# A gated cross-attention and expert layer: root steps of three norms on GpSimd, another order of A's transfers, another softmax path for pair 0, and sixteen leading products

## The chip, the cores and the metric

One core of a Trainium2 chip. The metric is the device time of one execution in microseconds (us), the median of three. Engines: TensorE (PE, with PEld for its weight loads), VectorE (DVE), ScalarE (ACT), GpSimd (POOL) and SyncE (SP), which here only issues transfers.

## The reference

For each of 16 batches x is 128 x 1024 (channels by positions) and ctx is 128 x 1024. What is computed:

```
xn  = layernorm(x)                      # over the 1024 positions
q   = Wq xn,  k = Wk ctx,  v = Wv ctx   # 8 heads of 64, hidden 512
qh  = softmax(q, over the 64 of a head) / 8
kh  = softmax(k, over the 1024 positions)
o   = Wo (heads: (kh v^T)^T qh) + bo
x  += tanh(g_xattn) * o / |o|_channels * g * sqrt(128)
y   = layernorm(x)
gates = softmax over the 16 largest of y Wr^T (64 experts), 0 elsewhere
x  += tanh(g_ffn) * 2 * sum_experts gates * B (A y)     # rank 16 each
```

All of it is float32 in accuracy: each product is made of three matmuls of float32r parts (high x high, low x high, high x low), so every matrix exists as a "hi" and a "lo" tile.

## The kernel before, in words

The program has two stages, with an order for each engine written out by hand; engines meet only at semaphores. The attention stage is a function `body(b, head, tail, ahead)` on every engine, called for b = 0 to 16: the "head" part works on batch b, the "tail" part ends batch b-1, and "ahead" loads and prepares batch b+1. Batches 0, 1, 14, 15 and 16 are written out, 2 to 13 are a loop (GpSimd splits its loop at 5 and 13). "Body 14" below is the call with b = 14. The second stage (`ffn_body`) takes the experts, one batch after another.

In a body TensorE makes k in four blocks of 128 hidden rows (`mm_k(b, 0..3)`, into banks 0 and 1) and q in four pairs of position blocks (`mm_q(b, 0..3)`, into banks 2 and 3). Each has one buffer, so the next product waits for the exponential of the one before. For k: VectorE takes the maximum (`max_k`, L868), ScalarE the exponential (`exp_k`, L586), TensorE transposes it (`tr_k`, L1284), ScalarE copies it to hi (L617) and VectorE makes lo (`lo_k`, L895). For q the softmax is over 64 neighbours, with 16 maxima to a pair (`max_q`, L874). A pair in `SHIFTED` (1 and 2 before) gets its maxima subtracted by two matmuls of the identity with the negated maxima, added onto q in PSUM (`shift_q`, L1274), and then one exponential of 128x1024 (L595). The other pairs (0 and 3 before) get 16 exponentials of 128x64, each with its maximum as bias (L602). GpSimd then halves the rows (`halve`, L391), VectorE sums (`sum_q`, L879), GpSimd multiplies (`normalise`, L398), TensorE transposes (`tr_q`, L1293), ScalarE and VectorE make hi and lo (L610, L888).

The tail: `context(b-1)` (24 matmuls of ekT by ctxT), copied to hi by ScalarE (`hi_kc`, L623) and lo by VectorE (`lo_kc`, L900), `fold` (12 matmuls of 128x256 with the folded Wv and Wo), `scale_m` (L912), `mt_hi`, `mt_lo` on GpSimd (L476), and `output` (two halves of 12 matmuls). The order on TensorE in a body before:

```
context(b-1, 0); mm_q(b, 0); context(b-1, 1); mm_k(b, 1); shift_q(b, 0)
tr_q(b-1, 1); fold(b-1); mm_q(b, 1); mm_k(b, 2); tr_k(b, 0); output ...
```

(`shift_q(b, 0)` did nothing, as pair 0 was not shifted.) On ScalarE the first 8 exponentials of pair 0 stood before `hi_kc`, the other 8 behind it.

The norms |o| of a batch are found from squares: the norms of batches 0 to 2 together, in body 14. TensorE sums them (`sum_early`), then VectorE takes an inverse root in 11 steps on 128x96 tiles (`early_norms`, L846 to L854: a clamp, a bit trick for the first guess, 3 Newton rounds of 3), spread over body 14 in five places. `spread` (L864) broadcasts the roots, GpSimd multiplies and adds (`spread_first` L436, `add_first` L446). For later batches VectorE does the same on 128x32 tiles in the second stage (`norm_u`).

For the second stage the weights are loaded while the attention ends: A's high parts by eight converting transfers of 544 KB on GpSimd's queue (`hi_a`, L419; t = 0 to 2 in body 15, 3 and 4 at its end, 5 to 7 in body 16 behind `halve(15, 3)`), over buffers of the attention stage, so t >= 3 waits for the last q product and the last transpose of k. B's parts (`b_raw`, L311, L316), u and x come on SP's queue, also in body 16. The first product of the second stage, `up(0, 0)` (L60 to L62, aT by yT), stands in body 16 behind `fold(15)` and waits for all of A and for `lo_y(0)` (L1013). `lo_y(0)` waits for `add_first(1)`.

Of the kernel before, what the change touches and what calls it, by code (L numbers as in the profile page):

```python
# [6 lines left out]
def flamingo_layer(nc, x, ctx, ctxT, g_xattn, g_ffn, WqT, WkT, Wv, WoT, bo, g, AT, BT, u_dram, out):  # L7
# [8 lines left out]
    NB, C, N = x.shape  # L16
# [24 lines left out]
    SHIFTED = (1, 2)  # L41
# [45 lines left out]
    with outer:  # L87
# [126 lines left out]
        n_part, n_sum, n_step, n_spread = sem("n_part"), sem("n_sum"), sem("n_step"), sem("n_spread")  # L214
        u_done, x2_done = sem("u_done"), sem("x2_done")
# [133 lines left out]
        def _(pool):  # L349
# [80 lines left out]

            def spread_first(e):
# [25 lines left out]
            def body(b, head, tail, ahead, split=False):  # L457
# [4 lines left out]
                if tail and not head:  # L462
                    for t in range(5, DC):
                        hi_a(t)
# [13 lines left out]
                if split:  # L478
                    lo_a(b - SPLIT)
                if head and not ahead:  # L480
                    add_first(0)
# [17 lines left out]
                if head and not ahead:  # L499
                    add_first(1)  # L500
                if head:
                    halve(b, 2)
                if head and not ahead:
                    for t in range(3, 5):
                        hi_a(t)

# [40 lines left out]
        def _(act):  # L547
# [42 lines left out]
            def exp_q(b, p, halves=(0, 1)):  # L590
# [8 lines left out]
                for h in halves:  # L599
# [89 lines left out]
            def body(b, head, tail, ahead, early=False):  # L689
# [6 lines left out]
                if head and started(b):  # L696
                    exp_q(b, 0, (0,))
# [5 lines left out]
                if head:  # L703
# [5 lines left out]
                    exp_q(b, 0, (1,) if started(b) else (0, 1))  # L709
# [98 lines left out]
        def _(dve):  # L808
# [48 lines left out]
            def early_norms(steps):  # L857
                for k in steps:
                    norm_step(k, 1, psN_early.rearrange("p (e n) -> p e n", e=EARLY), EARLY, 0)

            def spread(slot, dst, steps):

                dve.wait_ge(n_step, steps)
# [176 lines left out]
            def norm_u(e):  # L1040

                before = NRT * (e - EARLY + 1)
# [3 lines left out]
                spread(0, rb, before + NRT)  # L1046
# [13 lines left out]
            def body(b, head, tail, ahead, early=False):  # L1060
# [9 lines left out]
                if last:  # L1070
                    dve.wait_ge(ctx_lo, 2 * NB)
                    spread(0, rb_first[0], NRT)
                if ahead and started(b):
                    stats(b + 1)
                if head and started(b):
                    max_q(b, 0)
                if tail:
                    sum_q(b - 1, 3)
                if early:
                    part_early(b - 2)  # L1080
                if ahead and started(b):
                    std(b + 1, range(5))
# [477 lines left out]
```

## Time and profile before

| | |
|---|---|
| median of 3 runs | 977.32 us (974.84, 977.32, 977.46) |
| the profiled execution, its own time | 975.75 us |
| its span, first to last instruction | 974.1 us |
| mean granted TensorE clock | 0.992 |
| busy: PE, DVE, ACT, POOL | 928.2, 708.3, 531.6, 464.9 us |
| attention stage with the change-over, until the first product of the second stage | about 566 us |
| one body in the loop | 33.0 us |

Busy times are sums over the span and do not say what a stage waits for; for that the timelines of one body and the waits are read. A matmul's own duration is modelled to its end, and the next one starts before it: the distance of two starts is what one costs.

### The profile page before, as it was taken

The page shows a single profiled execution, that of the slowest core. Times are in us where ns is not written, and L with a number is a line of the kernel's source. Part 1 is how long each engine was busy: PE and PEld are TensorE (multiplying, and loading weights), DVE is VectorE, ACT ScalarE, POOL GpSimd, SP SyncE. Part 2 cuts the span into 40 slices and gives each one's busy share as a digit, 9 for nine tenths or more (in the row PEclk, how much of TensorE's full clock was granted, in tenths as well). Part 3 has the DMA queues.
Part 4 walks back from the last instruction along what each step waited for, and adds up shares of the span by engine and source line. Part 5 has one row for each costly group of instructions (what it writes and reads, how often), then busy time and mean ns, then how long its engine had stood idle before and what let it go on. Part 6 is the DMA issues. An engine that isn't in the chain of part 4 may idle for free.

```text
span 974.1 us, 16214 instructions
## 1 busy us (share of the span) xinstructions
PE 928.2 (95%) x5036; PEld 790.3 (81%) x5036; DVE 708.3 (73%) x1541; ACT 531.6 (55%) x1214; POOL 464.9 (48%) x311
## 2 busy tenths in 40 slices
PE   4899999999999999999989779999999999999998
PEld 3687777788887878787858679999999999999986
DVE  5888888878888888888897738766666666666621
ACT  5888887788878887887867624222222222222100
POOL 3665656677777867785757824311111111111100
PEclk9999999999999999999999989999999999999999
DMA  4216221232223122311311754111111111111001
GB/s 151 87 65 233 103 104 47 87 131 72 101 87 131 65 93 103 131 65 46 127 62 51 252 231 151 66 65 66 65 66 67 65 65 65 64 58 51 22 22 43
DMA packets 24805, 88.30 MB, mean 91 GB/s; under 512 B 3264, under 2 KB 3264, under 8 KB 24768
## 3 DMA queue, kind: packets, MB, share of 16 engines
q1 hardware_dynamic: 19296, 67.91, 19.1%
q0 software_dynamic: 5184, 19.40, 6.1%
q10 hardware_dynamic: 288, 0.52, 0.2%
q8 instruction: 20, 0.33, 0.1%
q14 instruction: 17, 0.14, 0.0%
HBM read 71.04 MB, written 16.78 MB: 90 GB/s over the span
## 4 chain that ended last, share of the span: by engine, by line
PE 64%; DVE 15%; ACT 10%; issue 8%; POOL 1%; DMA 1%; DVEq 0%; ACTq 0%; POOLq 0%
PE ps L60 18%; PE ps L62 18%; PE ps L61 18%; ACT qe L602 7%; PE ps L1284 3%; PE ps L1293 3%; DVE kmax L868 3%; DVE qT_lo L888 2%; DVE qtop L874 2%; DVE ekT_lo L895 2%; PE ps L1387 1%; PE ps L1358 1%; DVE mt L912 1%; DVE std_t L81 1%; ACT qT_hi L610 1%
## 5 line engine op out<-in xcount | busy, mean ns | idle before, releaser
L452 POOL TENSOR_TENSOR rb<-u_in,rb 128x1024 f32<-128x1024 f32 x14 | 33.7, 2408 | 260.1 <-DVE rb L864 260.1
L398 POOL TENSOR_TENSOR qe<-qe,qrec 128x1024 f32<-128x1024 f32 x64 | 121.3, 1905 | 54.5 <-DVE qrec L882 54.5
L60 PE MATMUL ps<-aT_hi,yT_hi 128*128 128x448 f32 (+2 forms) x384 | 128.2, 334 | 9.0 <-issue 9.0
L62 PE MATMUL ps<-aT_lo,yT_hi 128*128 128x448 f32 (+2 forms) x384 | 126.5, 329 | 0.0
L61 PE MATMUL ps<-aT_hi,yT_lo 128*128 128x448 f32 (+2 forms) x384 | 126.4, 329 | 0.0
L602 ACT ACTIVATE qe<-ps,qtop 128x64 f32<-128x64 f32 x512 | 111.3, 377 | 27.6 <-DVE qtop L874 27.6
L888 DVE TENSOR_TENSOR qT_lo<-ps,qT_hi 128x512 fp32r<-128x512 f32 x128 | 82.5, 686 | 51.8 <-ACT qT_hi L610 51.3
L391 POOL TENSOR_TENSOR qhalf<-qe 128x512 f32<-128x512 f32 x64 | 82.0, 1282 | 69.5 <-ACT qe L602 69.3
L60 PE MATMUL ps<-bT_hi,hT_hi 128*128 128x512 f32 x256 | 102.5, 400 | 0.0
L62 PE MATMUL ps<-bT_lo,hT_hi 128*128 128x512 f32 x256 | 99.9, 390 | 0.0
L61 PE MATMUL ps<-bT_hi,hT_lo 128*128 128x512 f32 x256 | 99.7, 390 | 0.0
L682 ACT ACTIVATE hT_hi<-ps 128x512 fp32r<-128x512 f32 x32 | 19.1, 597 | 143.8 <-PE ps L1387 143.8
L617 ACT ACTIVATE ekT_hi<-ps 128x512 fp32r<-128x512 f32 x128 | 70.5, 607 | 31.7 <-PE ps L1284 31.3
L586 ACT ACTIVATE ek<-ps,kmax 128x1024 f32<-128x1024 f32 x64 | 72.7, 1135 | 20.6 <-DVE kmax L868 20.6
L610 ACT ACTIVATE qT_hi<-ps 128x512 fp32r<-128x512 f32 x128 | 69.6, 598 | 24.0 <-PE ps L1293 24.0
L60 PEld LDWEIGHTS ps<-aT_hi,yT_hi 128*128 128x128 f32 x384 | 73.0, 190 | 11.6 <-issue 9.2
L895 DVE TENSOR_TENSOR ekT_lo<-ps,ekT_hi 128x512 fp32r<-128x512 f32 x128 | 81.2, 676 | 1.0 <-ACT ekT_hi L617 1.0
L868 DVE TENSOR_REDUCE kmax<-ps 128x1 f32<-128x1024 f32 x64 | 77.5, 1210 | 1.9 <-PE ps L62 1.9
L1293 PE MATMUL ps<-ident,qe 128*128 128x128 f32 x512 | 69.7, 278 | 6.6 <-DVE ekT_lo L895 6.0
L1293 PEld LDWEIGHTS ps<-ident,qe 128*128 128x128 f32 x512 | 58.0, 141 | 21.7 <-issue 12.2
L61 PEld LDWEIGHTS ps<-aT_hi,yT_lo 128*128 128x128 f32 x384 | 73.1, 190 | 2.3
L62 PEld LDWEIGHTS ps<-aT_lo,yT_hi 128*128 128x128 f32 x384 | 73.0, 190 | 2.0
(148 smaller groups left out, 2358.6 us busy)
## 6 DMA issues: line engine op xcount, KB each, us to landing
x_in<-in_x SPq DMA_DIRECT2D x16, 512.0 KB, 4.4
ctx_in<-in_ctx SPq DMA_DIRECT2D x16, 512.0 KB, 4.9
ctxT_in<-in_ctxT SPq DMA_DIRECT2D x16, 512.0 KB, 3.3
ctxT_hi<-in_ctxT POOLq DMA_DIRECT2D x16, 512.0 KB, 3.7
u_scratch<-osb SPq DMA_DIRECT2D x16, 512.0 KB, 3.8
out<-res SPq DMA_DIRECT2D x16, 512.0 KB, 2.8
x<-in_x SPq DMA_DIRECT2D x15, 512.0 KB, 3.9
u_in<-u_scratch SPq DMA_DIRECT2D x14, 512.0 KB, 3.2
```

Of the source, the lines that this page charges most:

```text
L60: nc.tensor.matmul(psum, whi, mhi, start=start, stop=False)
L61: nc.tensor.matmul(psum, wlo, mhi, start=False, stop=False)
L62: return nc.tensor.matmul(psum, whi, mlo, start=False, stop=stop)
L391: nc.gpsimd.tensor_tensor(qhalf[:, p % 2, :].rearrange("p (h d) -> p h d", d=DH // 2), v[:, :, 0:DH // 2], v[:, :, DH // 2:DH], ALU.add).t ...
L398: nc.gpsimd.tensor_tensor(v, v, w, ALU.mult).then_inc(q_norm, 1)
L586: nc.scalar.activation(ek[:, j % 2, :].rearrange("p (a n) -> p a n", a=HF), psK, ACT.Exp, bias=kmax[:, j:j + 1], accum_out=ksum[:, j:j + 1 ...
L602: last = nc.scalar.activation(qe[:, p, HD * h + DH * n:HD * h + DH * n + DH], psQ[:, h, v], ACT.Exp, bias=qtop[:, p % 2, H * h + n:H * h + ...
L610: nc.scalar.activation(qT[0][:, :, n * P:n * P + P], psT[:, h, :].rearrange("p (j n) -> p j n", n=P), ACT.Copy).then_inc(q_hi, 1)
L868: nc.vector.tensor_reduce(kmax[:, j:j + 1], psK, axis=AX.XY, op=ALU.max, negate=True).then_inc(k_max, 1)
L888: nc.vector.tensor_tensor(qT[1][:, :, v], psT[:, h, :].rearrange("p (j n) -> p j n", n=P), qT[0][:, :, v].bitcast(f32), ALU.subtract).then ...
L895: nc.vector.tensor_tensor(ekT[1][:, n, w], psT[:, h, :].rearrange("p (n d) -> p n d", d=P), ekT[0][:, n, w].bitcast(f32), ALU.subtract).th ...
L1293: last = nc.tensor.transpose(psT[:, h, j * P:j * P + P], qe[:, p, w:w + P], ident[:, :])
```

## The change

- Pair 0 joins the shifted pairs: two matmuls and one 128x1024 exponential instead of 16 small ones; pair 3 alone keeps the bias form. On TensorE both halves of `context(b-1)` now stand together at the head of a body, before `mm_q(b, 0)`; `shift_q(b, 0)` now works, behind `mm_k(b, 1)`. On VectorE `max_q(b, 0)` moves from before `sum_q(b-1, 3)` to behind `lo_kc(b-1)`; in body 16 `lo_kc(15)` moves ahead of `sum_q(15, 3)`; `part_early` stands before the first `std` steps.
- The early root: VectorE makes the clamp and the first guess in one place, and GpSimd the three rounds, 4 steps each (12 steps on 128x96), behind `mt_lo` of body 14 and ahead of `normalise(14, 0)`. `spread` waits for these. GpSimd's body 14 is now written out.
- A's transfers 3 to 7 are issued together at the end of GpSimd's body 15, and `add_first(1)` comes behind them instead of before `halve(15, 2)`.
- TensorE's program begins with 16 matmuls of the identity with itself, 128x512 each, into a bank that is not yet used.

```
-    SHIFTED = (1, 2)
+    WARM = 16
+    SHIFTED = (0, 1, 2)
GpSimd:
+            def early_newton():
+                s, r, t = ns[:, :, :], nr[:, :, :], nt[:, :, :]
+                pool.wait_ge(n_guess, 2)
+                for k in range(4 * NEWTON):
+                    if k > 0:
+                        pool.wait_ge(n_newton, k)
+                    if k % 4 == 0:
+                        last = nc.gpsimd.tensor_tensor(t, r, s, ALU.mult)
+                    elif k % 4 == 1:
+                        last = nc.gpsimd.tensor_tensor(t, t, r, ALU.mult)
+                    elif k % 4 == 2:
+                        last = nc.gpsimd.tensor_scalar(t, t, -0.5, 1.5, ALU.mult, ALU.add)
+                    else:
+                        last = nc.gpsimd.tensor_tensor(r, r, t, ALU.mult)
+                    last.then_inc(n_newton, 1)
...
-                if tail and not head:
-                    for t in range(5, DC):
-                        hi_a(t)
...
+                if isinstance(b, int) and b == NB - 2:
+                    early_newton()
...
-                if head and not ahead:
-                    add_first(1)
                 if head:
                     halve(b, 2)
                 if head and not ahead:
-                    for t in range(3, 5):
+                    for t in range(3, DC):
                         hi_a(t)
+                    add_first(1)
...
-            with pool.Fori(SPLIT + DC, NB - 1) as b:
+            with pool.Fori(SPLIT + DC, NB - 2) as b:
                 body(b, head=True, tail=True, ahead=True)
+            body(NB - 2, head=True, tail=True, ahead=True)
ScalarE:
-                if head and started(b):
-                    exp_q(b, 0, (0,))
                 if tail:
                     hi_kc(b - 1)
...
-                    exp_q(b, 0, (1,) if started(b) else (0, 1))
+                    exp_q(b, 0)
VectorE:
+            def early_guess():
+                s, r = ns[:, :, :], nr[:, :, :]
+                dve.wait_ge(n_sum, 1)
+                nc.vector.tensor_scalar(s, psN_early.rearrange("p (e n) -> p e n", e=EARLY), MIN_SS, None,
+                                        ALU.max).then_inc(n_guess, 1)
+                dve.wait_ge(n_guess, 1)
+                first_root(r, s).then_inc(n_guess, 1)
...
-                if head and started(b):
-                    max_q(b, 0)
-                if tail:
-                    sum_q(b - 1, 3)
                 if early:
                     part_early(b - 2)
-                if ahead and started(b):
-                    std(b + 1, range(5))
-                if norms:
-                    early_norms(range(2))
-                if tail:
-                    lo_kc(b - 1)
+                if norms:
+                    early_guess()
+                if ahead and started(b):
+                    std(b + 1, range(5))
+                if tail and head:
+                    sum_q(b - 1, 3)
+                if tail:
+                    lo_kc(b - 1)
+                if tail and not head:
+                    sum_q(b - 1, 3)
                 if head and started(b):
+                    max_q(b, 0)
                     max_k(b, 1)
...
-                if norms:
-                    early_norms(range(2, 4))
-                if norms:
-                    early_norms(range(4, 7))
...
TensorE:
                 if tail:
                     context(b - 1, 0)
+                    context(b - 1, 1)
                 if head:
                     if not started(b):
                         pe.wait_ge(wq_low, 1)
                     mm_q(b, 0)
-                if tail:
-                    context(b - 1, 1)
-                if head:
                     mm_k(b, 1)
                     shift_q(b, 0)
...
             pe.wait_ge(id_ready, 3)
+            for k in range(WARM):
+                nc.tensor.matmul(psX[:, 0, :], ident_r[:, :], ident_r[:, :].unsqueeze(1).broadcast_to([P, 4, P]),
+                                 start=True, stop=True)
```

The counts of semaphores are changed to fit (`n_guess`, `n_newton`; `norm_u` and `sum_u` no longer count the early steps).

## Rows read from the trace of the kernel before

**Rows 1.** The page, part 1: busy us (share of the span) x instructions.

```profile
PE 928.2 (95%) x5036; PEld 790.3 (81%) x5036; DVE 708.3 (73%) x1541; ACT 531.6 (55%) x1214; POOL 464.9 (48%) x311
```

**Rows 2.** Windows by stage: one loop body, body 14, body 15, start of body 16.

```profile
308.00:341.00 33.00, 32.41 (x178) 26.64 (x177) 27.70 (x49) 26.78 (x68) 24.70 (x18) 1.00 0.27 96
...
473.60:512.90 39.30, 34.06 (x179) 26.79 (x178) 36.39 (x60) 27.42 (x68) 21.73 (x15) 0.99 0.27 91
...
512.90:546.50 33.60, 31.95 (x171) 26.29 (x170) 27.95 (x46) 25.20 (x64) 26.01 (x18) 0.97 0.20 68
...
546.50:565.80 19.30, 9.21 (x55) 7.74 (x54) 11.74 (x30) 9.77 (x26) 12.03 (x11) 0.84 1.04 360
```

**Rows 3.** Timeline of the start: start us, us, engine line op [idle before <-releaser].

```profile
1.32 0.29 POOL L352 TENSOR_SCALAR_AFFINE_SELECT ident<-ident 128x128 f32<-128x128 f32 x1 [0.24 <-POOL ident L350]
...
9.72 0.77 PE L60 MATMUL ps<-ctx_hi,wk_hi 128*128 128x512 f32 x1 [9.72 <-POOL ctx_lo L362]
...
16.77 0.42 PE L62 MATMUL ps<-ctx_lo,wk_hi 128*128 128x512 f32 x1
...
17.42 3.39 ACT L602 ACTIVATE qe<-ps,qtop 128x64 f32<-128x64 f32 x16 [1.46 <-DVE qtop L874]
...
21.96 0.50 PE L60 MATMUL ps<-ctx_hi,wk_hi 128*128 128x512 f32 x1
```

**Rows 4.** Groups of instructions by line: busy us, mean ns.

```profile
L595 ACT ACTIVATE qe<-ps 128x1024 f32<-128x1024 f32 x32 | 33.0, 1030 | 0.0
```

**Rows 5.** Timelines of the loop body with b = 9: PE, ACT, DVE.

```profile
308.33 0.49 PE L60 MATMUL ps<-ekT_hi,ctxT_hi 128*128 128x512 f32 x1
...
312.38 0.50 PE L60 MATMUL ps<-wq_hi,xn_hi 128*128 128x512 f32 x1 [0.37 <-ACT qe L602]
...
319.47 0.28 PE L62 MATMUL ps<-wvo_lo,kc_hi 128*128 128x256 f32 x1
...
316.23 0.65 ACT L623 ACTIVATE kc_hi<-ps 128x512 fp32r<-128x512 f32 x1
...
313.38 1.23 DVE L874 TENSOR_REDUCE qtop<-ps 128x16 f32<-128x1024 f32 x1 [1.09 <-PE ps L62]
...
316.91 0.69 DVE L900 TENSOR_TENSOR kc_lo<-ps,kc_hi 128x512 fp32r<-128x512 f32 x1 [0.59 <-ACT kc_hi L623]
...
319.90 1.40 DVE L912 TENSOR_TENSOR mt<-ps,krec 64x512 f32<-64x512 f32 x2
```

**Rows 6.** The chain of waits in the loop: start us, us, what.

```profile
331.82 0.43 PE ps L1274 x2
```

**Rows 7.** Timelines of body 14: PE, DVE, POOL.

```profile
502.48 1.17 PE L1284 MATMUL ps<-ident,ek 128*128 128x128 f32 x8 [1.47 <-DVE qT_lo L888]
...
511.50 1.72 PE L1293 MATMUL ps<-ident,qe 128*128 128x128 f32 x8 [2.86 <-DVE ekT_lo L895]
...
498.83 2.32 DVE L854 SCALAR_TENSOR_TENSOR nr<-nt,nr 128x96 f32<-128x96 f32 x1
...
487.24 1.28 POOL L476 TENSOR_TENSOR mt_lo<-mt,mt_hi 128x512 fp32r<-128x512 f32 x1 [2.05 <-ACT mt_hi L627]
...
492.23 1.90 POOL L398 TENSOR_TENSOR qe<-qe,qrec 128x1024 f32<-128x1024 f32 x1 [3.71 <-DVE qrec L882]
...
494.94 2.52 POOL L362 TENSOR_TENSOR ctx_lo<-ctx_in,ctx_hi 128x512 fp32r<-128x512 f32 x2 [0.27 <-ACT ctx_hi L562]
...
498.66 2.37 POOL L375 TENSOR_TENSOR ctxT_lo<-ctxT_in,ctxT_hi 128x1024 fp32r<-128x1024 f32 x1
```

**Rows 8.** Timelines of the change-over: POOL, DVE, PE.

```profile
549.48 1.14 POOL L419 DMA_DIRECT2D aT_hi<-in_AT  x2
...
553.43 1.64 POOL L419 DMA_DIRECT2D aT_hi<-in_AT  x3
...
556.13 1.28 DVE L1013 TENSOR_TENSOR yT_lo<-ps,yT_hi 128x512 fp32r<-128x512 f32 x2
...
565.82 0.71 PE L60 MATMUL ps<-aT_hi,yT_hi 128*128 128x448 f32 x1 [9.05 <-issue]
```

More of the change, by code:

```diff
@@ L214, in flamingo_layer @@
         n_part, n_sum, n_step, n_spread = sem("n_part"), sem("n_sum"), sem("n_step"), sem("n_spread")
+        n_guess, n_newton = sem("n_guess"), sem("n_newton")
         u_done, x2_done = sem("u_done"), sem("x2_done")
@@ L588, in exp_k, with exp_q @@
                                      accum_out=ksum[:, j:j + 1]).then_inc(k_exp, 1)
-            def exp_q(b, p, halves=(0, 1)):
+            def exp_q(b, p):
                 if started(b):
@@ L598, in exp_q @@
                 act.wait_ge(q_max, 4 * b + p + 1)
-                for h in halves:
+                for h in range(2):
                     for n in range(H):
@@ L855, in norm_step, with spread @@
                 last.then_inc(n_step, 1)
[L857 to L863, printed above, removed]
+            def early_guess():
[5 more added lines that the diff above has]
+                first_root(r, s).then_inc(n_guess, 1)
+            def spread(slot, dst, *done):
+                dve.wait_ge(*done)
                 nc.vector.transpose(dst[:, :], nr[:, slot, :].unsqueeze(2).broadcast_to([P, N // 32, 32])).then_inc(n_spread, 1)
@@ L1040, in norm_u @@
             def norm_u(e):
-                before = NRT * (e - EARLY + 1)
+                before = NRT * (e - EARLY)
                 for k in range(NRT):
@@ L1045, in norm_u @@
                 dve.wait_ge(x2_done, e)
-                spread(0, rb, before + NRT)
+                spread(0, rb, n_step, before + NRT)
             stats(0)
@@ L1071, in body @@
                     dve.wait_ge(ctx_lo, 2 * NB)
-                    spread(0, rb_first[0], NRT)
+                    spread(0, rb_first[0], n_newton, 4 * NEWTON)
                 if ahead and started(b):
                     stats(b + 1)
+                if early:
+                    part_early(b - 2)
+                if norms:
[8 more added lines that the diff above has]
+                    sum_q(b - 1, 3)
                 if head and started(b):
                     max_q(b, 0)
-                if tail:
-                    sum_q(b - 1, 3)
-                if early:
-                    part_early(b - 2)
-                if ahead and started(b):
-                    std(b + 1, range(5))
-                if norms:
-                    early_norms(range(2))
-                if tail:
-                    lo_kc(b - 1)
-                if head and started(b):
                     max_k(b, 1)
@@ L1090, in body @@
                     dve.wait_ge(xn_lo, 2 * NB)
-                    spread(1, rb_first[1], NRT)
+                    spread(1, rb_first[1], n_newton, 4 * NEWTON)
                 if ahead and started(b):
@@ L1134, in body @@
                     dve.wait_ge(q_T, 8 * NB)
-                    spread(2, rb, NRT)
+                    spread(2, rb, n_newton, 4 * NEWTON)
                 if tail:
@@ L1147, in body @@
                     lo_k(b, 2)
-                if norms:
-                    early_norms(range(7, 10))
                 if last:
@@ L1154, in body @@
                     lo_k(b, 3)
-                if norms:
-                    early_norms(range(10, NRT))
                 if last:
@@ L1314, in fold @@
                 if isinstance(b, int) and b == NB - 3:
-                    pe.wait_ge(n_step, 1)
+                    pe.wait_ge(n_guess, 1)
                 for j in range(CH):
@@ L1344, in sum_u @@
                 pe.wait_ge(n_part, e + 1)
-                pe.wait_ge(n_step, NRT * (e - EARLY + 1))
+                if not (isinstance(e, int) and e == EARLY):
+                    pe.wait_ge(n_step, NRT * (e - EARLY))
                 nc.tensor.matmul(psN, sel[:, :, :].rearrange("p q n -> p (q n)"), part[:, 0, :],
```

## The prediction, made before the changed kernel was run

> **What bounds the kernel now.** First the page's busy times: TensorE is busy for 95% of the span [rows 1], so little can be won where it is full, and much where it is not. Then the windows by stage [rows 2]: a loop body of 33.0 us holds 32.4 us of busy TensorE; body 14 takes 39.3 us, 6.3 more than a loop body, with TensorE busy for 34.1; body 15 takes 33.6 at a granted clock of 0.97; the 19.3 us from the start of body 16 hold 9.2 us of TensorE work. Then timelines of the places with gaps: the start [rows 3], one loop body [rows 5, 6], body 14 [rows 7], the change-over [rows 8]. The second stage behind 565.8 us is not touched; it only moves with its start.
>
> **Part 1, the leading products.** The identity is ready at about 2.0 us (the select ends at 1.61 and one operation of its size follows) [rows 3]. TensorE's first real matmul starts at 9.72. Its early 128x512 products last 0.77 to 0.63 us and the first of 0.42 us comes at 16.77: it ran at the lower of its two levels (1.2 GHz) for 7.0 us of work. In these 7.05 us 14 products were issued, with about 1 us of waits, so 0.43 us apart; 16 take 6.9 us and end at about 8.9, ahead of 9.72: no delay. If the 6.9 us raise the level, the six q products of batch 0 take 1.4 us instead of 2.7: 1.3 gained. Between these 1.3 and nothing I take 1.3, since the work ahead is as long as the work that raised it before. Pair 0 shifted helps here too: the 16 exponentials last 3.39 us [rows 3] against 1.03 for one large [rows 4], with 0.43 of shift ahead: 1.9 less on ScalarE. Not all of it counts: the maximum of k block 1 stands behind the statistics of x(1) on VectorE, and I let k block 2 (before at 21.96) come 1.9 us earlier in all, 1.3 and 0.6. **Start: -1.9.**
>
> **Part 2, the loop body.** Before: context starts at 308.33; 15 products later the second half of q pair 0 starts at 312.38, behind a wait of 0.37 for the last exponential of pair 3; the last fold matmul starts at 319.47 [rows 5]: 11.14 us after the start. (308.33 to 312.38 less the wait gives 0.24 us a product, and 0.23 without switches.) After: 24 context products end issuing at 5.55, q pair 0 at 6.9, k block 1 at 8.3. The wait for pair 3 is gone, as its exponentials end near 4.0: -0.5. The shift adds 0.43 [rows 6]. Does the shift wait? Context's last result is there at 5.75; kc_hi takes 0.65, kc_lo 0.69, the maximum 1.23 [rows 5]: 8.35, just when TensorE gets there at 8.3. So the last fold starts at 11.1 to 11.25: nothing gained on TensorE. VectorE began `scale_m` at 319.90 while the last fold result came at 319.75 [rows 5], since its k maximum waited for ScalarE's half of pair 0 and `kc_hi`; that 0.1 to 0.15 goes. From there to the next body VectorE, then TensorE, set the pace as before. ScalarE loses 3.4 - 1.03 = 2.4 us of work per body, but it idles in front of kc_hi and is not what this stage waits for: 0. Per body between -0.25 and +0.15; I take -0.1, and 12 bodies give **-1.2**. Bodies 2 to 4 have `part_early` ahead of `max_q` now, which stood behind it: even.
>
> **Part 3, the root in body 14.** VectorE is busy 36.4 us in body 14 against 27.7 in a loop body [rows 2]: the 11 steps cost 8.7, as single ones lasted 2.32 us. TensorE stood 1.47 us at 502.48 and 2.86 us at 511.50 [rows 7], both behind VectorE work queued after the steps, and the body came to +6.3. After: 2 steps on VectorE, in a place where it waits for `kc_hi` or q anyway (0.6 to 1.1 us in rows 5): 0. GpSimd gets 12 steps. `mt_lo` ends at 488.5, `normalise(14, 0)` waited 3.71 us until 492.23 for VectorE [rows 7]: that is the cover. One step: from 1.28 us for 512 columns and 2.37 for 1024 [rows 7] 96 columns make 0.39, proportionally 0.24; between dependent steps 0.09 to 0.24 [rows 3]. So 12 steps cost 4.0 to 7.6 us; I take 5.8, 2.1 beyond the cover. Behind it on GpSimd stand `normalise(14, 0)`, a ctxT transfer (not urgent), ctx_lo of batch 15 (before 494.94 to 497.46 [rows 7]), halve, ctxT_lo. TensorE needs the second half of ctx_lo about 1.4 us after that, so 0.7 us of the lateness reaches it. Without cover the whole 5.8 would. -6.3 + 0.7 = **-5.6**. And the clock: the 2.86 us gap left body 15 at 0.97 of 33.6 us [rows 2], 1.0 us lost at the lower level; with no such gap, **-1.0**.
>
> **Part 4, the change-over.** `up(0, 0)` started at 565.82, although `lo_y(0)` was done at 557.4 [rows 8]: it waited for A's last transfer, issued by 555.1. Now 3 to 7 go out together behind `halve(15, 2)`, without `add_first(1)` (2.4 us) ahead of it: from 549.48 - 2.4 = 547.1, five at 0.57 us, to 550.0, 5 us earlier for the last one. But the transfer engines are busy at a share of 1.04 from 546.5 to 565.8, with 360 GB/s [rows 2]: an earlier issue brings only the moments at which A's queue ran dry before (the transfers of 549.48 and those of 553.43 have 3 us between them [rows 8]), while B's loads on SP's queue start when they did. Bounds: 0, and 5 (the issue). I take 1.5, nearer to the full queue: **-1.5**. The rest moved costs nothing: `add_first(1)` ends at 552.4, its reader `lo_y(0)` at 556.13; `halve(15, 3)` is late by 0.2; `lo_kc(15)` ahead of `sum_q(15, 3)` lets fold start about 1 us earlier, in front of a wait for A, so 0. If A landed at once, `lo_y(0)` would be next, at 557.
>
> The Trainium skill, page "DMA: Bandwidth & Descriptors", section on queues, rings and completion order, says that each transfer engine goes round-robin between the queues that have work. By that, B's traffic takes its half as soon as it is issued, whatever waits in A's queue, and the gain of part 4 would be near 0 instead of 1.5.
>
> **Sum.** -1.9 - 1.2 - 5.6 - 1.0 - 1.5 = -11.2 against the profiled execution's 975.75: 964.5. The median of the runs, 977.32, lies 1.6 higher, and an execution of the new kernel may do likewise; I say 965.0. A difference under 0.3% (2.9 us) can hardly be told from none.
>
> **Rivals.**
>
> (a) A's queue was starved, not the engines: the issue counts in full, and `up(0, 0)` comes 4 to 8 us earlier, bounded by `lo_y(0)` at 557.4. For it: the 2.8 us between the two issues [rows 8], a queue of two transfers in between. Against: busy share 1.04. Time 958 to 962. Chance 0.18.
>
> (b) The small parts give nothing: the level has fallen back by 9.72 or did not rise (+1.3), the shift of pair 0 waits 0.2 us more for its maximum in each body (+2.6), A gives 0 (+1.5). The change then doesn't do at the start what it says. Time 967 to 972. Chance 0.15.
>
> (c) GpSimd's steps are held by VectorE. The row of 2.32 us at 498.83 ends with GpSimd's 2.37 us from 498.66 [rows 7]: the two hold each other. If each of 12 steps is held for a VectorE operation of 1.2 us, they take some 15 to 20 us, 12 to 16 beyond the cover, and ctx_lo(15) is late by as much: the 6.6 us of part 3 are given back. Time 973 to 978. Against: VectorE's work there reads PSUM, and GpSimd's 128x512 steps last 1.28 us throughout, beside any neighbour. Chance 0.04.
>
> The Trainium skill, page "SBUF — State Buffer", section "SBUF: two separate sides", says that VectorE and GpSimd share a port pair as an exclusive lock, for VectorE operations with two SBUF inputs or in a two-port mode; this rule is what (c) would rest on, and the row at 498.83 agrees with it.
>
> (d) Slower: the shift of pair 0 as a new wait in every body. `max_q` now stands behind `kc_lo`, and so behind context, `kc_hi` and the sums; what is behind the shift on TensorE (transposes, fold) and everything after fold comes late with it. Parts 1, 3 and 4 give 10.0, so with 14 bodies it decides from 0.7 us a body, and is slower by 0.3% from 0.95 us: 980 to 984. It needs `kc_hi` 1 us later than I count, by ScalarE. Against: ScalarE ends pair 3 near 4.0, 1.7 us ahead of context's end. Chance 0.03.
>
> **Numbers.** Forecast 0.60 (963 to 967). Faster: 0.60 + 0.18 + 0.15 = 0.93, less 0.01 for the upper end of (b) and unnamed cases: 0.92. Same: 0.05, from (c) and the weak ends. Slower: 0.03. Range 959 to 970.5: it takes in most of (a) and (b), with step costs of 4.0 to 7.6 us (-0.7 to +1.8) and the 1.6 us between executions.
>
> **What would show it.** Right: the first real products last 0.4 us; k block 2 starts at about 20; body 14 from context to context is 33 to 34.5 us and no wait of TensorE behind VectorE in it is over 1 us; body 15 has clock 1.00; GpSimd's 12 steps fill 4 to 7.6 us; a loop body is 32.9; `up(0, 0)` comes 17.5 to 18.5 us after the start of body 16 (19.3 before). ScalarE's busy sum falls by some 38 us (16 x 2.4) with no effect of its own. Wrong: a wait before L1274 of over 0.3 us in each body; `up(0, 0)` within 14 us of body 16; GpSimd steps of over 1 us.

## The result, and the profile after

The changed kernel took 959.71 us (median of 4 runs, 959.63 to 961.45) beside 977.39 us for the kernel before on the same chip (4 runs, 974.84 to 978.66): ratio 0.9827, 95% interval 0.9804 to 0.9849. Against the forecast of 965.0 it is faster by 5.3 us more, inside the range of 959 to 970.5 near its lower end, and among the times that rival (a) gave. The profiled execution took 959.67 us, span 957.9; that of before 975.75 and 974.1. So 16.1 us are to be found between the two traces, where the sum found 11.2.

The page of the changed kernel, part 1, and the group that answers to [rows 4] (busy us, mean ns, idle before):

```profile
PE 932.2 (97%) x5084; PEld 800.5 (84%) x5084; DVE 704.0 (73%) x1532; ACT 492.2 (51%) x974; POOL 469.5 (49%) x323
...
L613 ACT ACTIVATE qe<-ps 128x1024 f32<-128x1024 f32 x48 | 49.3, 1027 | 47.8 <-PE ps L1288 47.7
```

Beside [rows 1], ScalarE has 39.4 us less to do (240 instructions fewer), and the large exponential is there 48 times instead of 32. TensorE has 48 matmuls more, the 16 leading ones and two for each shift of pair 0. None of that says where the time went. That comes from the starts of the bodies, the first context matmul of each:

| stretch | before | after | difference | predicted |
|---|---|---|---|---|
| start to the first context matmul | 40.51 | 38.86 | -1.65 | -1.9 |
| body 1 | 32.93 | 32.64 | -0.29 | -0.1 |
| bodies 2 to 4 | 102.75 | 101.54 | -1.21 | 0 |
| bodies 5 to 13 | 297.43 | 295.98 | -1.45 | -0.9 |
| body 14 | 39.26 | 33.03 | -6.23 | -5.7 |
| body 15 | 33.65 | 33.36 | -0.29 | -1.1 |
| body 16 to `up(0, 0)` | 19.29 | 14.27 | -5.02 | -1.5 |
| the rest | 408.28 | 408.22 | -0.06 | 0 |

(The -0.1 of part 2 is in ten of the plain bodies and in bodies 14 and 15.)

Windows of the changed kernel, in the columns of [rows 2] (start:end, length, busy us and count of PE, PEld, DVE, ACT, POOL, then granted clock, DMA share, GB/s):

```profile
30.00:35.00 5.00, 4.62 (x17) 3.91 (x18) 3.85 (x9) 3.07 (x7) 4.53 (x3) 0.66 0.25 79
304.50:337.40 32.90, 32.69 (x179) 27.11 (x179) 28.01 (x49) 24.47 (x53) 24.77 (x18) 1.00 0.27 97
469.00:502.05 33.05, 32.55 (x181) 26.99 (x180) 29.03 (x51) 24.04 (x53) 25.65 (x27) 1.00 0.25 80
502.05:535.40 33.35, 31.43 (x175) 25.95 (x174) 27.91 (x46) 23.16 (x50) 26.66 (x19) 1.00 0.30 100
535.40:549.70 14.30, 8.90 (x56) 7.74 (x54) 10.47 (x25) 8.59 (x25) 11.63 (x11) 0.90 1.08 386
```

The loop body is 32.9 as forecast. Body 14 is now one like the others: VectorE has 29.0 us of work instead of 36.4. Body 15 has clock 1.00 as forecast, and yet gained little. In the last window the DMA share is still about 1 (1.08, from 1.04), but the rate went from 360 to 386 GB/s. The first row is new: a stretch at a mean clock of 0.66 in batch 0, where the kernel before kept 1.00. The kernel before had its own lower stretch from 511.6 to 515.0, behind the 2.86 us wait of body 14.

The start, timeline of TensorE in the changed kernel (start us, us, engine, line, operation, idle before and its releaser):

```profile
2.05 6.43 PE L1494 MATMUL ps<-ident_r 128*128 128x512 f32 x16 [2.05 <-POOL ident_r L358]
9.22 0.47 PE L61 MATMUL ps<-ctx_hi,wk_hi 128*128 128x512 f32 x1 [0.75 <-POOL ctx_lo L364]
...
12.72 0.47 PE L61 MATMUL ps<-wq_hi,xn_hi 128*128 128x512 f32 x1 [1.39 <-POOL xn_lo L384]
...
19.56 0.51 PE L61 MATMUL ps<-ctx_hi,wk_hi 128*128 128x512 f32 x1 [0.36 <-ACT ek L604]
```

The 16 products last 6.43 us (predicted 6.9) and end 0.75 us before the first real one, which lasts 0.47 instead of 0.77. K block 2 starts at 19.56 (before 21.96, predicted about 20). 0.5 us of that are no gain of the change: the first real product has its data at 9.22 instead of 9.72 here, since the first loads landed earlier in this execution.

The loop body of the changed kernel that starts at 304.52, timelines of TensorE and VectorE:

```profile
312.93 0.70 PE L1288 MATMUL ps<-qmax,ident_r 128*128 128x512 f32 x2
...
315.65 0.28 PE L63 MATMUL ps<-wvo_lo,kc_hi 128*128 128x256 f32 x1
...
310.96 0.65 DVE L921 TENSOR_TENSOR kc_lo<-ps,kc_hi 128x512 fp32r<-128x512 f32 x1
311.65 1.23 DVE L895 TENSOR_REDUCE qmax<-ps 128x16 fp32r<-128x1024 f32 x1
...
315.97 1.41 DVE L933 TENSOR_TENSOR mt<-ps,krec 64x512 f32<-64x512 f32 x2 [0.50 <-PE ps L63]
```

The shift of pair 0 (L1288 here, L1274 before) starts 8.41 us into the body without a wait: it was put at 8.3 to 8.35. The last fold matmul starts at 11.13, where it started at 11.14 before. `scale_m` (`mt`) starts at 11.45 instead of 11.57: the 0.12 us that the body gains. It is the last fold result that it waits for now, no longer VectorE's own queue.

GpSimd in body 14 of the changed kernel:

```profile
483.02 1.28 POOL L492 TENSOR_TENSOR mt_lo<-mt,mt_hi 128x512 fp32r<-128x512 f32 x1 [2.02 <-ACT mt_hi L645]
484.26 0.39 POOL L441 TENSOR_TENSOR nt<-nr,ns 128x96 f32<-128x96 f32 x1
484.73 0.39 POOL L443 TENSOR_TENSOR nt<-nt,nr 128x96 f32<-128x96 f32 x1
485.21 0.27 POOL L445 TENSOR_SCALAR nt<-nt 128x96 f32<-128x96 f32 x1
...
489.10 0.39 POOL L447 TENSOR_TENSOR nr<-nr,nt 128x96 f32<-128x96 f32 x1
489.45 1.90 POOL L400 TENSOR_TENSOR qe<-qe,qrec 128x1024 f32<-128x1024 f32 x1
...
491.92 2.52 POOL L364 TENSOR_TENSOR ctx_lo<-ctx_in,ctx_hi 128x512 fp32r<-128x512 f32 x2
```

The 12 steps fill 484.26 to 489.45, 5.2 us (estimate 5.8, bounds 4.0 to 7.6). Nine of them last 0.39 us and three 0.27, with 0.08 to 0.09 between, and none is held by VectorE; `normalise(14, 0)` follows at once. On VectorE single steps of this size had lasted up to 2.32 us [rows 7]. The timeline of VectorE in body 14 of the kernel before shows when:

```profile
492.30 1.95 DVE L852 SCALAR_TENSOR_TENSOR nt<-nt,nr 128x96 f32<-128x96 f32 x1
...
501.48 0.26 DVE L852 SCALAR_TENSOR_TENSOR nt<-nt,nr 128x96 f32<-128x96 f32 x1
```

The same step lasts 1.95 us beside GpSimd's `normalise` of 492.23 [rows 7] and 0.26 where GpSimd stood, from 501.03 to 505.09. Of the nine Newton steps there, the four without a GpSimd operation beside them last 0.20 to 0.26 us, the five others 1.04 to 2.32.

The change-over, GpSimd, VectorE and TensorE of the changed kernel:

```profile
530.91 1.65 POOL L421 DMA_DIRECT2D aT_hi<-in_AT  x3
...
535.64 2.72 POOL L421 DMA_DIRECT2D aT_hi<-in_AT  x5
538.32 2.44 POOL L465 TENSOR_TENSOR x<-x_second,u_first 128x1024 f32<-128x1024 f32 x1
...
544.42 1.28 DVE L1034 TENSOR_TENSOR yT_lo<-ps,yT_hi 128x512 fp32r<-128x512 f32 x2
...
549.68 0.71 PE L61 MATMUL ps<-aT_hi,yT_hi 128*128 128x448 f32 x1 [5.40 <-issue]
```

The last of A's transfers is issued 3.0 us into body 16 (before 8.5), and `up(0, 0)` starts at 14.27. `lo_y(0)` ends at 10.3 (545.70), so A is still what is late. The prediction named "within 14 us" as the sign that part 4 was judged wrongly, and 14.27 sits beside it.

### The profile page after: what moved, and what is told of

The parts are those of the page before. It is cut to its first block, busy times and chain, and to the rows that moved or that the text cites. A ratio compares the mean times of both kernels' runs of the same rounds, so it can differ in the third digit from the quotient of the medians.

```text
span 957.9 us, 16074 instructions
## 1 busy us (share of the span) xinstructions
PE 932.2 (97%) x5084; PEld 800.5 (84%) x5084; DVE 704.0 (73%) x1532; ACT 492.2 (51%) x974; POOL 469.5 (49%) x323
## 4 chain that ended last, share of the span: by engine, by line
PE 81%; DVE 10%; issue 5%; ACT 1%; POOL 1%; DMA 1%; DVEq 0%; ACTq 0%; POOLq 0%
PE ps L61 22%; PE ps L63 22%; PE ps L62 22%; PE ps L1307 6%; PE ps L1298 4%; DVE qT_lo L909 3%; PE ps L1288 2%; PE ps L1402 1%; PE ps L1373 1%; DVE mt L933 1%; DVE ekT_lo L916 1%; DVE qmax L895 1%; DVE bn L831 1%; DVE kmax L889 1%; DVE qsum L900 1%
## 5 line engine op out<-in xcount | busy, mean ns | idle before, releaser
L635 ACT ACTIVATE ekT_hi<-ps 128x512 fp32r<-128x512 f32 x128 | 70.1, 607 | 32.9 <-PE ps L1298 32.5
L604 ACT ACTIVATE ek<-ps,kmax 128x1024 f32<-128x1024 f32 x64 | 72.3, 1130 | 13.4 <-DVE kmax L889 13.4
L613 ACT ACTIVATE qe<-ps 128x1024 f32<-128x1024 f32 x48 | 49.3, 1027 | 47.8 <-PE ps L1288 47.7
```

The lines of the kernel that those rows point to most:

```text
L604: nc.scalar.activation(ek[:, j % 2, :].rearrange("p (a n) -> p a n", a=HF), psK, ACT.Exp, bias=kmax[:, j:j + 1], accum_out=ksum[:, j:j + 1 ...
L635: nc.scalar.activation(ekT[0][:, 4 * h:4 * h + 4, j * P:j * P + P], psT[:, h, :].rearrange("p (n d) -> p n d", d=P), ACT.Copy).then_inc(k_ ...
```

## The experiments

Kernels made from the kernel before have its line numbers, the others those of the changed kernel or up to four more. Three sets were timed, each beside its own runs of the kernel before: 974.93 us (15 runs) for those on A's order and B, 974.25 (19 runs) for the leading products, the bias and the root, 976.42 (7 runs) for the last four. A ratio is always to the kernel before of the same set.

### The order of A's transfers

Undone in the changed kernel, GpSimd's program:

```diff
+                if tail and not head:
+                    for t in range(5, DC):
+                        hi_a(t)
...
+                if head and not ahead:
+                    add_first(1)
                 if head:
                     halve(b, 2)
                 if head and not ahead:
-                    for t in range(3, DC):
+                    for t in range(3, 5):
                         hi_a(t)
-                    add_first(1)
```

> The changed kernel with A's transfers and add_first(1) in their old places (3 and 4 at the end of GpSimd's body 15, 5 to 7 in body 16). In the trace of the changed kernel up(0,0) started 14.3 us after the start of body 16 against 19.3 before. If the order of the transfers made these 5.0 us: up(0,0) at 18.5 to 19.5 us into body 16 and a time of 964 to 965 us. If the earlier kc_lo and fold or the smoother bodies 14 and 15 made them: 14 to 15 us and 960 us.

The reverse, this order alone put into the kernel before:

> The kernel before with nothing but the new order of A's transfers and add_first(1). If the gain belongs to this part alone: up(0,0) at 14 to 15 us into body 16 (19.3 before), bodies 1 to 15 as before, time 971 to 973 us. My prediction's reading (transfer engines full, gain 1.5): 17.8 us and 976 us.

Undone: 962.82 us (2 runs), ratio 0.9876 (0.9809 to 0.9942). `up(0, 0)` starts 17.51 us into body 16; the changed kernel has 14.27, and 14.10 in a second profile. Alone: 971.84 us (8 runs), ratio 0.9969 (0.9949 to 0.9989), so 3.1 us, and `up(0, 0)` at 15.88 where the kernel before has 19.29. TensorE with the order undone:

```profile
552.91 0.71 PE L61 MATMUL ps<-aT_hi,yT_hi 128*128 128x448 f32 x1 [8.59 <-issue]
```

TensorE with the order alone:

```profile
561.61 0.71 PE L60 MATMUL ps<-aT_hi,yT_hi 128*128 128x448 f32 x1 [5.66 <-issue]
```

At `up(0, 0)` the two directions give 3.2 and 3.4 us: twice what I took for part 4, and within its bounds of 0 and 5. Both starts lie outside the ranges expected (18.5 to 19.5 undone, 14 to 15 alone).

That they agree so well is partly luck, because each of the four profiles has another tail. The packets of A (4352 bytes each) show it: all but the last 16 had ended 16.4 us into body 16 in the kernel before and 12.0 with the order alone, 16.3 with the order undone and 11.7 in the changed kernel. So the order moves the main part by 4.4 to 4.6 us, and the rest of the change by 0.1 (16.4 to 16.3). The last 16 packets then took 2.3, 3.4, 0.7 and 1.9 us. The DMA view of the kernel with the order alone, for the 3.2 us from 558.3 to 561.5, just before `up(0, 0)`:

```profile
q1 hardware_dynamic: 351, 1.29, 99.0%
q0 software_dynamic: 12, 0.04, 3.3%
```

A's queue (q0) has 12 packets left there, and the other queue, with B, has the engines.

Where does the earlier end come from? One half is in the DMA view, for the stretch from 5 to 10 us into body 16. The kernel before:

```profile
DMA packets 389, 1.51 MB, mean 302 GB/s; under 512 B 41, under 2 KB 41, under 8 KB 389
## 3 DMA queue, kind: packets, MB, share of 16 engines
q0 software_dynamic: 371, 1.48, 97.2%
```

The changed kernel:

```profile
DMA packets 506, 1.95 MB, mean 391 GB/s; under 512 B 57, under 2 KB 57, under 8 KB 506
...
q0 software_dynamic: 501, 1.94, 109.8%
```

A's queue fills the engines' time in both, to 97% and 110%. But in the kernel before 302 GB/s are moved, and in the changed one 391. The share of busy time was taken in the prediction as proof that nothing faster was to be had. It is none; the recorded time of a packet seems to hold time in which it moves nothing (argued from the two rates, not measured apart). The number of transfers outstanding does not explain the rate either. In the kernel before, four of A's transfers had been issued and had not landed from 555.1 to 556.5, and the engines moved

```profile
DMA packets 92, 0.39 MB, mean 277 GB/s; under 512 B 3, under 2 KB 3, under 8 KB 92
```

while in the changed kernel, with only the last two left, from 545.4 to 546.4 they moved

```profile
DMA packets 105, 0.43 MB, mean 426 GB/s; under 512 B 7, under 2 KB 7, under 8 KB 105
```

What lowers the rate with the old order stays open. The second half of the mechanism is B. In the kernel before, from 556.5 to 562.5:

```profile
DMA packets 635, 2.42 MB, mean 404 GB/s; under 512 B 61, under 2 KB 61, under 8 KB 634
...
q1 hardware_dynamic: 342, 1.28, 55.9%
q0 software_dynamic: 292, 1.14, 50.6%
```

As soon as B's loads flow, each queue has about half. The Trainium skill, page "DMA: Bandwidth & Descriptors", section "Queues, rings and completion order", says that an engine goes round-robin between the queues that have work, and the trace agrees (55.9% and 50.6%). Its consequence was drawn wrongly in the prediction: sharing does not make an earlier issue worthless, since what A moves before B starts need not be shared (the changed kernel moved 391 GB/s there).

B held back in the kernel before tests that half by itself:

```diff
+            sp.wait_ge(a_ready, 16 * DC)
             for k in range(KC // 2):
                 sp.dma_start(b_raw[:, k, :], BT[k])
```

> The kernel before with SP waiting for all of A before it issues B's loads; u(2) is still issued ahead. Sharing theory: 1.5 MB of A were left when B's loads began 9.5 us into body 16, and alone they go at over 0.4 MB/us: up(0,0) at 14 to 15.5 us (19.3 before), time 971 to 973. If the late issue of transfers 5 to 7 alone set the landing, B's loads did not matter: 18.5 to 19.3 and 975 to 977.

`up(0, 0)` came at 15.14 us into body 16 instead of 19.29. The tail is short here, 0.6 us for the last 16 packets. In time it was 973.61 us (8 runs), ratio 0.9981 (0.9959 to 1.0002), so no gain is shown, against 4 us at that one place. The profiled execution keeps what the transfer gives: behind `up(0, 0)` it takes 408.0 us, as the kernel before does (408.3), and its time of 970.7 us is the lowest of the eight. The others go up to 976.1, and no trace shows what they lose. Holding B is no proven substitute for the order.

Last in this group, `add_first(1)` ahead of the transfers again, but all five together:

```diff
+                if head and not ahead:
+                    add_first(1)
                 if head:
                     halve(b, 2)
                 if head and not ahead:
                     for t in range(3, DC):
                         hi_a(t)
-                    add_first(1)
```

> The changed kernel with add_first(1) back ahead of halve(15,2): five transfers together still, but issued 2.4 us later. Depth theory (the rate of A's queue hangs on how many transfers stand in it, and the first three keep it busy until about 4 us into body 16): a loss of 0 to 1 us, up(0,0) at 14.3 to 15.5. Issue theory (the moment of the last issue sets the landing): 16.7. Sharing theory (what of A is left when B's loads start goes at half speed): 16 to 18. Time 960 to 963.

Inconclusive. 963.14 us over two runs (965.6 in the profiled one and 960.69), ratio 0.9879 (0.979 to 0.9968). In the profile A's last packet ended 18.9 us into body 16 and `up(0, 0)` started at 19.41, though all but 16 packets had ended at 14.2. From 14.7 on they end one at a time, 0.33 us apart, which points at one of the 16 transfer engines, late and alone (argued from the spacing; the trace does not name the engines). In the other run there is no room for so long a wait. That tail differs between executions, and it is why a single profile misleads here. It was short, 0.5 to 0.6 us, in the two profiles in which B hardly ran beside A's end (B held, and A 0 to 2 early, below) and 0.7 to 4.7 in those of the others named here, so sharing with B may be what stretches it. The 5.0 us between the traces of the kernel before and the changed one are mostly order, 4.7 in the main part, as their tails are nearly the same (2.3 and 1.9).

### The leading products

Left out of the changed kernel:

```diff
-    WARM = 16
+    WARM = 0
```

> The changed kernel without the 16 leading products. If they raise TensorE's level before the first real product: here the first real products last 0.6 to 0.8 us again, context of batch 0 starts 1.0 to 1.5 us later (40.0 to 40.4 instead of 38.9) and the time is 961 us. If they only look good (the exponentials of pair 0 made the whole gain of the start): no difference over 0.3 us.

Alone in the kernel before:

```diff
             pe.wait_ge(id_ready, 3)
+            for k in range(16):
+                nc.tensor.matmul(psX[:, 0, :], ident_r[:, :], ident_r[:, :].unsqueeze(1).broadcast_to([P, 4, P]),
+                                 start=True, stop=True)
```

> The kernel before with nothing but the 16 leading products. Level theory: q products of batch 0 at 0.23 us apart, maximum and 16 exponentials 1.3 us earlier, context of batch 0 at 39.0 to 39.4 (40.5 before); time 976. No-effect theory: 40.5 and 977.

Without them: 960.99 us (2 runs), ratio 0.9845 (0.9791 to 0.9898). The first real matmul is at the lower level again, TensorE in this kernel:

```profile
9.10 0.77 PE L61 MATMUL ps<-ctx_hi,wk_hi 128*128 128x512 f32 x1 [9.10 <-POOL ctx_lo L364]
```

From the first q product to the first context matmul it takes 26.79 us (39.39 for the latter, where 40.0 to 40.4 was expected), the changed kernel 26.14 and the kernel before 27.29. So the products give 0.65 us, half of the 1.3 forecast, and pair 0 with the order the other 0.5. Both are readings of single profiles. Six more, of kernels with the same program for batch 0, have 26.37, 26.11, 26.15, 26.21, 25.40 and 25.41; the last two (the last two kernels of the table below) are the only ones in which the level does not fall in batch 0, and there it is 1.4 us, all that was forecast. In time the two runs do not set this kernel apart from the changed one.

Alone in the kernel before: 975.13 us (8 runs), ratio 0.9995 (0.9975 to 1.0015), no gain. TensorE there:

```profile
9.32 0.47 PE L60 MATMUL ps<-ctx_hi,wk_hi 128*128 128x512 f32 x1 [1.51 <-POOL ctx_lo L362]
...
19.17 0.50 PE L60 MATMUL ps<-wq_hi,xn_hi 128*128 128x512 f32 x1 [0.67 <-ACT qe L602]
...
19.81 0.63 PE L62 MATMUL ps<-wq_lo,xn_hi 128*128 128x512 f32 x1
20.27 0.79 PE L60 MATMUL ps<-ctx_hi,wk_hi 128*128 128x512 f32 x1
```

The level is up at 9.32 and down again from 19.8, behind waits of 1.38, 1.73 and 0.67 us in batch 0, and once more from 33.2 to 36.8 (granted clock 0.53). The first context matmul comes at 40.81, where it was at 40.51. What the products raise is lost again in batch 0, behind its gaps; in the changed kernel at 31.2. The step of rival (b), "the level has fallen back", was right in kind, only later than 9.72.

### Pair 0 by bias again

```diff
-    SHIFTED = (0, 1, 2)
+    SHIFTED = (1, 2)
```

> The changed kernel with pair 0 back in the form with bias (16 exponentials, no shift matmuls), the new order of everything kept. In the new order these 16 exponentials stand whole between kc_hi and exp_k(1). If the shift is what makes the new order bearable: kmax and with it exp_k(1), hi_q, hi_m come about 2.4 us later, and since VectorE waits for hi_q in its chain behind scale_m, a body takes 33.5 to 35 us instead of 32.9, time 968 to 990. If ScalarE has slack in this stage for it, as the prediction says (ScalarE is not what the stage waits for): 32.4 to 32.9 (0.43 of matmuls saved), time 954 to 960.

969.5 us (6 runs, 963.94 to 971.83), ratio 0.9938 (0.9904 to 0.9972). The loop bodies take 33.4 us, more than the changed kernel's 32.87 and more than the 33.0 before. ScalarE and TensorE in the body that starts at 310.61:

```profile
319.02 3.38 ACT L620 ACTIVATE qe<-ps,qtop 128x64 f32<-128x64 f32 x16 [2.02 <-DVE qtop L895]
322.17 1.23 ACT L604 ACTIVATE ek<-ps,kmax 128x1024 f32<-128x1024 f32 x1
...
322.45 0.50 PE L61 MATMUL ps<-wq_hi,xn_hi 128*128 128x512 f32 x1 [0.36 <-ACT qe L620]
```

The new order puts `max_q` behind `kc_lo`, so the 16 exponentials start later; the next exponential, `ek`, starts 11.56 us into the body instead of 10.44, and TensorE waits 0.36 us for ScalarE. The new order needs the shift; the shift in the old order was not run. Without the shift the order costs 0.4 us a body against the kernel before; with it, it gains 0.12. "ScalarE is not what this stage waits for: 0" was the right price for the change as a whole, but hid two terms of opposite sign, +0.4 and -0.5.

### Only the root on GpSimd

The kernel before with `early_guess` and `early_newton` in place of `early_norms`:

```diff
-                if norms:
-                    early_norms(range(2))
+                if norms:
+                    early_guess()
...
+                if isinstance(b, int) and b == NB - 2:
+                    early_newton()
```

> The kernel before with nothing but the root's three rounds on GpSimd. If the root steps on VectorE made body 14's 6.3 us: body 14 takes 33.0 to 33.7 us here, body 15 33.2 to 33.4 (the clock no longer falls, but mt_lo behind spread_first(0) takes its place), time 970.5. If it was something else of body 14: 35 us or more.

967.49 us (8 runs), ratio 0.9931 (0.9913 to 0.9948): 6.8 us by this part alone. Its body 14:

```profile
474.96:507.53 32.57, 32.14 (x178) 26.59 (x178) 28.22 (x51) 26.38 (x68) 25.55 (x27) 1.00 0.24 82
```

32.57 us, a little less than the changed kernel's 33.03. That is better than the 33.0 expected, and the time better than the 970.5. The body now costs nothing over the others, so no part of GpSimd's 5.2 us is seen at TensorE.

### Building on what was found

The changed kernel once more, for a fair pair, and three steps beyond it, each on top of the one before:

> The changed kernel again, as the measure for the three beside it: 958 to 961 us.

First A's transfers 0 to 2, which stood behind `spread_first(1)` late in body 15, go behind `halve(15, 1)`:

```diff
                 if head:
                     halve(b, 1)
+                if head and not ahead:
+                    for t in range(3):
+                        hi_a(t)
+                if head:
                     lo_c(b)
```

> The changed kernel with A's first three transfers issued behind halve(15,1) instead of behind spread_first(1), some 6.5 us earlier. If what bounds the change-over is still A's queue: 3 to 7 then find it empty, 2.8 MB at 0.42 MB/us land 9.5 to 10.5 us into body 16, and up(0,0) starts at 10.4 to 11.5 (14.3 before), when lo_y(0) is done; TensorE stands about 2 us instead of 5.4 and may keep its level: time 953 to 956.5. If B's loads or x(1) on SP's queue were what held A: 13.5 to 14.3, no gain.

Then `part_early`, which the change had put ahead of `max_q` in bodies 2 to 4, goes behind it:

```diff
-                if early:
-                    part_early(b - 2)
...
+                if early:
+                    part_early(b - 2)
                 if tail:
                     lo_q(b - 1, 3)
```

> As e9, and part_early stands ahead of lo_q(b-1,3), where VectorE waits about 1 us, instead of ahead of max_q. If it is part_early that makes bodies 2 to 4 0.9 us longer than the others: 33.0 us each instead of 33.8, 2.3 us less than e9, 951 to 954. If bodies 2 to 4 are longer for another reason (the squares on ScalarE): 33.5 to 33.8 and no gain.

Then `spread_first(0)`, in GpSimd's body 15, goes behind `mt_lo`:

```diff
-                if head and not ahead:
-                    spread_first(0)
...
+                if head and not ahead:
+                    spread_first(0)
```

> As e10, and spread_first(0) on GpSimd behind mt_lo of body 15 instead of ahead of it. If spread_first(0) is what took the place of the lost clock in body 15: the wait of 0.5 us for mt_lo is gone and body 15 takes 32.7 to 33.0 instead of 33.4; 0.4 to 0.7 us less than e10. If VectorE's extra work there sets it: 33.4.

| kernel | us (median of 4) | ratio to before | interval | `up(0, 0)` in body 16 |
|---|---|---|---|---|
| changed, again | 959.24 | 0.9821 | 0.9804 to 0.9837 | 14.10 |
| A 0 to 2 early | 954.27 | 0.9771 | 0.9755 to 0.9787 | 10.36 |
| and `part_early` later | 952.24 | 0.9755 | 0.9739 to 0.9771 | 10.36 |
| and `mt_lo` first | 952.31 | 0.9751 | 0.9735 to 0.9767 | 11.28 |

The first step gives 5.0 us. GpSimd and TensorE in it:

```profile
524.49 1.63 POOL L421 DMA_DIRECT2D aT_hi<-in_AT  x3
...
545.95 0.47 PE L61 MATMUL ps<-aT_hi,yT_hi 128*128 128x448 f32 x1 [1.47 <-DVE yT_lo L1036]
```

Now A has landed and `lo_y(0)` is last, the bound that the prediction named as next. And the gap is so short that the level stays up: the first product lasts 0.47 us, where it lasted 0.71; the granted clock is 1.00 from 545.9 to 553. Behind `up(0, 0)` this profile takes 406.6 us where the changed kernel, again, has 408.0: 1.4 us less, from the level, beside the 3.7 of earlier start. The second step shortens bodies 2 to 4 from 34.03, 33.73 and 33.79 to 33.54, 33.24 and 33.25. That takes away the wait for the maximum which the changed kernel has in each of them, for instance on TensorE:

```profile
114.81 0.70 PE L1288 MATMUL ps<-qmax,ident_r 128*128 128x512 f32 x2 [0.84 <-DVE qmax L895]
```

33.0 was expected, and 0.4 us per body over a loop body remain unexplained. In its profile TensorE's clock is 1.000 throughout, in batch 0 too, where the profile of the step before it had 0.50 from 13.4 to 16.8. So its first context matmul comes 1.1 us earlier, which is not the step's doing; the three bodies give 1.5 us in the profiles, and the medians differ by 2.0. The third step removes the wait that is next in body 15, seen in the changed kernel as

```profile
517.58 0.50 PE L61 MATMUL ps<-qT_hi,mt_hi 128*128 128x512 f32 x1 [0.50 <-POOL mt_lo L492]
```

and the body goes from 33.36 to 33.20 instead of 32.7 to 33.0. But `up(0, 0)` comes 0.9 us later and at the lower level, and no time is won. VectorE and TensorE there:

```profile
541.77 1.28 DVE L1036 TENSOR_TENSOR yT_lo<-ps,yT_hi 128x512 fp32r<-128x512 f32 x2
...
544.00 0.71 PE L61 MATMUL ps<-aT_hi,yT_hi 128*128 128x448 f32 x1 [2.35 <-DVE yT_lo L1036]
```

The profile puts the wait down to `lo_y(0)`, but that had ended at 543.05. The last of A's transfers landed at 543.91, 11.2 us into body 16: GpSimd issued the five from 0.12 us into the body on, where it had begun 1.35 us ahead of it. A is late again. The last two versions can't be told apart; they are 24 us (2.5%) under the kernel before and 7 us under the changed one.

## Why the prediction was right, and which terms were off

The direction, the mechanism and the order of the parts held; the time was 5.3 us too high, and the runs put most of it on part 4.

- **Part 1, the start:** -1.65 measured, -1.9 predicted, but with other contents: 0.65 for the level (1.3 predicted; 1.4 in the two profiles whose level does not fall in batch 0), 0.5 for pair 0 and the order (0.6), and 0.5 of an earlier landing that belongs to the execution. Between 1.3 and nothing I chose 1.3 because the work ahead was as long as what had raised the level before. The gaps of batch 0 that follow were not looked at, and there the level mostly falls again.
- **Part 2, the loop body:** right to 0.1 us at each point that it named, -0.13 a body where -0.1 was taken. "Even" for bodies 2 to 4 was wrong by 0.4 us each: there the change gained too, and the later place of `part_early` shows that another 0.5 was left. Over bodies 1 to 13 it was 2.95 us where 1.0 was taken.
- **Part 3, the root:** -6.2 for -5.6, and -6.8 alone. A step cost the 0.39 us that was scaled from 128x512. The 0.7 us of lateness did not reach TensorE. Rival (c), steps held by VectorE, has no trace.
- **Part 3, the clock of body 15:** -0.3 for -1.0. The clock did become 1.00, so the mechanism is right, but the kernel before had lost only 0.4 us to it in the first 9 us of the body: its first twelve context matmuls took 3.90 us instead of 2.85, and the wait of 0.38 for the last exponential of pair 3 fell away in return. The profile with B held has the same gap (2.87 us) and keeps its level; its body 15 takes 33.43 against 33.65, so the level itself costs some 0.2 us there (33.50 and 33.92 in two other profiles in which it fell), and 0.45 in body 14 (38.81 against 39.26). The term took all that the matmuls lose at the lower level as lost to the body. Part of what that gives is taken again by a wait of 0.50 for `mt_lo` (0.23 before), which GpSimd's `spread_first(0)` now delays. With that moved, 0.16 came back.
- **Part 4, the change-over:** the failed step is "the transfer engines are busy at a share of 1.04 [...] an earlier issue brings only the moments at which A's queue ran dry". Measured 3.1 us by the order alone (interval 1.1 to 5.0) and 3.2 to 3.4 at `up(0, 0)`, instead of 1.5; the main part of A comes 4.4 to 4.7 us earlier, with a tail that varies behind it. The queue moved 302 GB/s at a share of 1.00 and 391 at 1.11, so the share did not mean full engines. Rival (a) had this right, that the earlier issue counts nearly in full, but not why: its queue of only two transfers is not what lowers the rate.
- **Size of the sum:** 6.8 for the root, 3.1 for the order of A, 1.65 for the start and 2.95 for the bodies 1 to 13 are 14.5 us; the two profiles differ by 16.1, the ratio's interval gives 14.8 to 19.2. The largest difference is the order of A, 5.0 in the two profiles and 3.1 in time alone, with an interval that takes in both.

Left open: why A's queue moves less with the old order; what makes the tail of its transfers and why it varies; why bodies 2 to 4 stay 0.4 us over the others; and why holding B back gives 4 us at `up(0, 0)` but only 1.9 in the time by the ratio, with an interval that reaches from 4.0 to nothing.

## What to carry to other kernels

A busy share near 1 of the transfer engines does not say that they are full: read GB/s in the same stretch (391 instead of 302 here, at nearly the same share), and issue what is needed first before the other queue takes its half. Short steps on the engine that is already the pace (here 11 of 128x96 on VectorE) can cost much more than their own duration when long GpSimd operations run beside them; here GpSimd, with a wait in front of its next operation, took them for nothing. A wait that the profile puts down to one engine can be for a transfer: compare the end of the named operation with the landing. And when a wait is removed, look for the next one at once, because it may be the cheapest gain left: moving three transfers 6.6 us earlier in body 15 was worth another 5.0 us.

## What was unexpected in the hardware

- The same 16 transfer engines, at a busy share of 1.00 to 1.11, moved 302 GB/s in one order of issue and 391 in the other, and 404 with two queues flowing. The number of transfers outstanding did not go with it: 277 GB/s with four, 426 with two.
- The granted clock does not show the level at the start: from 9.0 to 24.0 us the windows of the kernel before give 1.00, while its 128x512 products last 0.61 to 0.77 us until 16.3. The trace has no record of the clock there before 16.8 us. At this place only the duration of one product tells.
- The same gap need not lower the level. Behind 2.82 to 2.87 us in body 14 it fell in the kernel before, with the order alone and with the products alone, and stayed up with B held.
- GpSimd took a 128x96 product in 0.39 us and a scale with add in 0.27, next to VectorE work, without delay. The same size had cost VectorE 0.20 to 0.26 us alone and up to 2.32 beside a GpSimd operation of 2.37.
